# A decoder layer on one core: self-attention's output projection as three float32r products, in two parts around the transpositions, with values and query units in another order

## The reference

```
# self-attention: 16 query heads of 128, one key/value head, causal, rotary
xn = layernorm(x) * gamma                        # x: (32, 56, 256)
q  = rotary(xn @ Wq) * 128 ** -0.5               # 16 heads of 128
k, v = rotary((xn @ Wkv)[..., :128]), (xn @ Wkv)[..., 128:]
x2 = x + softmax(causal(q @ k.T)) @ v @ Wo       # Wo: (2048, 256), the projection changed here
# cross-attention: 16 heads of 16 over 1500 masked rows, then its own projection
x3 = x2 + norm(cross(layernorm(x2), context)) ...
# feed-forward: three quantised products, 256 -> 1024 (two, gated) -> 256
```

## Time and profile before

| | |
|---|---|
| median of three runs | 1445.63 us |
| the profiled execution | 1444.34 us |
| its span, first to last instruction | 1442.4 us |
| mean granted TensorE clock | 0.980 of full speed |
| TensorE busy | 1376.7 us |
| VectorE busy | 1013.8 us |
| ScalarE busy | 716.9 us |
| GpSimd busy | 447.3 us |

### The profile page before, as it was taken

How to read it: one execution, slowest core, us unless ns; L and a number is a source line. 1 busy time by engine, 2 the same in 40 slices (tenths; PEclk the granted TensorE clock), 3 DMA queues, 4 the chain that set the end, 5 groups by cost and what they waited for, 6 DMA issues and landing times.

```text
span 1442.4 us, 54968 instructions
## 1 busy us (share of the span) xinstructions
PE 1376.7 (95%) x25094; PEld 1176.8 (82%) x25094; DVE 1013.8 (70%) x1792; ACT 716.9 (50%) x939; POOL 447.3 (31%) x400
## 2 busy tenths in 40 slices
PE   5899999998899999999999999999999999999983
PEld 5687787786688888888888888888888888888872
DVE  4676676666136787786777777687878778677765
ACT  3445445444255645555555555555554555555540
POOL 4332333222222333333324233233333333332400
PEclk9999999999899999999999999999999999999995
DMA  9100001000111121111112121111212121121100
GB/s 260 23 1 31 1 1 31 1 30 1 58 49 57 31 77 44 56 58 46 58 37 63 31 77 52 57 49 45 64 31 77 41 62 55 45 61 34 49 2 7
DMA packets 38808, 66.75 MB, mean 46 GB/s; under 512 B 3605, under 2 KB 36818, under 8 KB 38578
## 3 DMA queue, kind: packets, MB, share of 16 engines
q1 hardware_dynamic: 38578, 63.24, 15.1%
HBM read 61.40 MB, written 1.84 MB: 44 GB/s over the span
## 4 chain that ended last, share of the span: by engine, by line
PE 71%; DVE 2%; issue 0%; POOL 0%; POOLq 0%; DVEq 0%
PE proj_ps L1277 19%; PE proj_ps L1268 19%; PE score_ps L1295 14%; PE sum_ps L1315 12%; PE side_ps L1350 2%; PE side_ps L1332 2%; PE side_ps L1364 1%; PE side_ps L1357 1%; PE side_ps L1339 0%; DVE inv L1109 0%; DVE exps L1097 0%; DVE amax L1150 0%; DVE hidden L1182 0%; DVE hidden L1193 0%; DVE sig L1192 0%
## 5 line engine op out<-in xcount | busy, mean ns | idle before, releaser
L1049 ACT ACTIVATE exps<-score_ps 125x1792 f32<-125x1792 f32 x192 | 320.5, 1669 | 419.0 <-PE score_ps L1295 419.0
L1097 DVE TENSOR_SCALAR exps<-exps,top 125x896 f32<-125x896 f32 x384 | 287.9, 791 | 18.0 <-ACT exps L1049 17.5
L1295 PE MATMUL score_ps<-spread,keys 32*125 32x112 f32 x6144 | 219.3, 279 | 0.0
L1315 PEld LDWEIGHTS sum_ps<-exps,vals 125*32 125x32 f32 x12288 | 163.0, 110 | 50.9 <-issue 34.4
L1088 DVE COPY vals<-proj_ps 125x512 f32<-125x512 f32 x192 | 128.2, 687 | 103.4 <-PE proj_ps L1277 103.0
L1295 PEld LDWEIGHTS score_ps<-spread,keys 32*125 32x125 f32 x6144 | 185.1, 183 | 15.4 <-issue 0.4
L1315 PE MATMUL sum_ps<-exps,vals 125*32 125x56 f32 x12288 | 191.5, 214 | 2.9 <-DVE exps L1097 2.9
L992 POOL TENSOR_TENSOR low<-raw_early,high 128x500 fp32r<-128x500 f32 x64 | 100.8, 1583 | 231.2 <-issue 115.4
L992 POOL TENSOR_TENSOR low_early<-raw_early,high_early 128x500 fp32r<-128x500 f32 x62 | 104.3, 1691 | 172.3 <-issue 104.1
L1041 ACT ACTIVATE keys<-proj_ps,b_k 128x500 f32<-128x500 f32 x192 | 129.9, 677 | 52.4 <-PE proj_ps L1268 52.4
L286 POOL TENSOR_TENSOR swapped<-swapped,sin 128x448 f32<-128x448 f32 (+1 forms) x72 | 88.6, 1232 | 138.5 <-ACT swapped L507 138.5
(11 more groups left out here) (156 smaller groups left out, 2411.6 us busy)
## 6 DMA issues: line engine op xcount, KB each, us to landing
raw_early<-in_ctxT SPq DMA_DIRECT2D x64, 500.0 KB, 4.0
raw<-in_ctxT SPq DMA_DIRECT2D x32, 500.0 KB, 3.5
w_q<-in_attn_Wq SPq DMA_DIRECT2D x4, 512.0 KB, 8.1
w_o<-in_attn_Wo SPq DMA_DIRECT2D x1, 2048.0 KB, 21.5
out<-y_out SPq DMA_DIRECT2D x16, 112.0 KB, 1.9
rows<-in_x SPq DMA_DIRECT2D x1, 1344.0 KB, 16.8
raw_early<-in_ffn_gate_wT SPq DMA_DIRECT2D x1, 1024.0 KB, 9.6
raw_early<-in_ffn_val_wT SPq DMA_DIRECT2D x1, 1024.0 KB, 5.1
```

The lines of the kernel that those rows point to most:

```text
L1049: nc.scalar.activation(exps[t % 2][:, :, :, :].rearrange("p h r n -> p r h n"), score_ps[0:TILE, :, 0:2 * QW].rearrange("p r (h n) -> p r ...
L1097: nc.vector.tensor_scalar(tile, tile, LIMIT_LO, top[:, n, at:at + 1], ALU.max, ALU.min)\
L1295: ins = nc.tensor.matmul(score_ps[0:TILE, r, to:to + HE * S], keys[c % 2][32 * r:32 * r + 32, k, (at + half) * TILE:(at + half + 1) * TILE ...
L1315: ins = nc.tensor.matmul(sum_ps[32 * h:32 * h + VW, g, :], vals[c % 2][:, at + half, HJ * g + h, :], exps[t % 2][:, half, r, col:col + S], ...
```

## The change

The output projection is computed from two parts of each operand. ScalarE copies `out_ps` to `outT_h` in float32r; VectorE subtracts that from `out_ps` and writes the rest as `outT_l` (`out_low`, four a pair). The weights are split in the same way into `w_oh` and `w_ol`, in two halves of eight heads, through the buffer that later holds the feed-forward weights (`out_weights`). `out_rows` then issues three float32r products for each head, 48 in all, and in the pairs with query units the first eight heads come ahead of `turn(p,0)` and the other eight behind it.

The order in a pair is new. `norm_turn`, q2 and q3 come behind `turn(p,1)` on TensorE; on ScalarE both `out_half(p,0,·)` and `probs_out(p,1)` come ahead of `normed_out` and the swaps of q2 and q3; on VectorE the first two `out_low` come ahead of q2's rotation. Pair 0 keeps q2 and q3 ahead of its transpositions.

To make room in SBUF, `masked` is gone (the masked scores are written into `probs`), there are three `swapped` buffers instead of four, `w_f` lies in the first half of `raw_early` and is loaded and split at pair 13 instead of 15, and five tiles of the feed-forward part are allocated and loaded in `block_b` (their reader waits for `late_in`). The diff, cut to its core:

```diff
-        w_o = sb("w_o", [P, AH, D])
+        w_oh = sb("w_oh", [P, AH, D], F32R)
+        w_ol = sb("w_ol", [P, AH, D], F32R)
...
-        masked = sb("masked", [P, AU, 2, S])
-        outT = sb("outT", [P, AH, ROWS])
+        outT_h = sb("outT_h", [P, AH, ROWS], F32R)
+        outT_l = sb("outT_l", [P, AH, ROWS], F32R)
...
             units += more[0:1]
             if p >= 2:
                 units += [("xq", p - 2)]
-            if j and g + 2 < GROUPS:
-                units += [("norm", g + 2)]
             units += more[1:2]
             if p in TOTALS:
                 units += [("total", TOTALS.index(p))]
             if p:
                 units += [("y", p - 1)]
+            if j and g + 2 < GROUPS:
+                units += [("norm", g + 2)]
             units += more[2:4]
             if p:
...
+            def out_weights(n):
+                sp.dma_start(w_raw[:, :].rearrange("p (h n) -> p h n", h=half_o),
+                             dram["attn_Wo"].rearrange("(h p) n -> p h n", p=P)[:, half_o * n:half_o * (n + 1), :])\
+                  .then_inc(wo_in[n], 16)
+
+            out_weights(0)
             sp.dma_start(w_xq[:, :, :], dram["xattn_WqT"].rearrange("(c p) n -> p c n", p=P)).then_inc(small2_in, 16)
             sp.dma_start(b_xq[:, :], dram["xattn_bq"]).then_inc(small2_in, 16)
+            sp.wait_ge(w_o_split, 1)
+            out_weights(1)
+            sp.wait_ge(early_zero, 2)
+            for to, of in early.loads(dram):
+                sp.dma_start(to, of).then_inc(early_in, 16)
+            sp.wait_ge(w_o_split, 2)
             for n, (src, how, _) in enumerate(W):
                 if n:
                     sp.wait_ge(raw_used, n)
                 c = src.shape[0] // P
                 sp.dma_start(w_raw[:, :].rearrange("p (c n) -> p c n", c=c), src.rearrange(how, p=P))\
                   .then_inc(raw_in[n], 16)
-                if n == 0:
-                    for k, name in enumerate(("xattn_WkT", "xattn_WvT")):
-                        sp.dma_start(early.w_f[:, k, :, :], dram[name].rearrange("(c p) n -> p c n", p=P))\
-                          .then_inc(early_w_in, 16)
-                    sp.wait_ge(early_zero, 2)
-                    for to, of in early.loads(dram):
-                        sp.dma_start(to, of).then_inc(early_in, 16)
             sp.wait_ge(raw_used, 3)
+            for k, name in enumerate(("xattn_WkT", "xattn_WvT")):
+                sp.dma_start(early.w_f[:, k, :, :], dram[name].rearrange("(c p) n -> p c n", p=P)).then_inc(early_w_in, 16)
+            sp.wait_ge(early_w_split, 2)
             for c in range(2):
                 sp.dma_start(early.ring(c), context_chunk(dram, c)).then_inc(early_ctx_in[c], 16)
...
+            def out_low(p, k, b):
+
+                dve.wait_ge(outT_high, 2 * (2 * p + k) + b + 1)
+                nc.vector.tensor_tensor(outT_l[:, AU * k:AU * (k + 1), b * S:(b + 1) * S],
+                                        out_ps[:, b, 0:AU * S].rearrange("p (h s) -> p h s", s=S),
+                                        outT_h[:, AU * k:AU * (k + 1), b * S:(b + 1) * S].bitcast(F32),
+                                        ALU.subtract).then_inc(outT_ready, 1)
+
+            def out_weights(n):
+
+                dve.wait_ge(w_o_high, n + 1)
+                nc.vector.tensor_tensor(w_ol[:, half_o * n:half_o * (n + 1), :].rearrange("p h n -> p (h n)"), w_raw[:, :],
+                                        w_oh[:, half_o * n:half_o * (n + 1), :].rearrange("p h n -> p (h n)").bitcast(F32),
+                                        ALU.subtract).then_inc(w_o_split, 1)
 
             def residual(p):
...
+            out_weights(0)
...
                 normalise(p)
                 for name in more[1:2]:
                     rotary(name)
+                if p == 0:
+                    out_weights(1)
                 if j == 0 and g + 2 < GROUPS:
...
+                if p == WEIGHTS_AT:
+                    early.weights_low(nc, dve, early_w_high, early_w_split)
                 if p:
                     residual(p - 1)
-                for name in more[2:3]:
+                for name in more[2:3] if p == 0 else ():
+                    rotary(name)
+                for b in range(2):
+                    out_low(p, 0, b)
+                for name in more[2:3] if p else ():
                     rotary(name)
                 if p:
                     norm2_rows(p - 1)
                 for name in more[3:4]:
                     rotary(name)
+                for b in range(2):
+                    out_low(p, 1, b)
                 if j and g + 2 < GROUPS:
                     rotary(("kv", g + 2))
...
-                if r >= 4:
-                    act.wait_ge(rot_ready, r - 3)
-                nc.scalar.copy(swapped[r % 4][0:64, 0:w], bank(name)[64:128, 0:w])
-                ins = nc.scalar.copy(swapped[r % 4][64:128, 0:w], bank(name)[0:64, 0:w])
+                if r >= 3:
+                    act.wait_ge(rot_ready, r - 2)
+                nc.scalar.copy(swapped[r % 3][0:64, 0:w], bank(name)[64:128, 0:w])
...
             def out_half(p, k, b):
 
                 act.wait_ge(pv_done, 2 * p + k + 1)
-                ins = nc.scalar.copy(outT[:, AU * k:AU * (k + 1), b * S:(b + 1) * S],
-                                     out_ps[:, b, 0:AU * S].rearrange("p (h s) -> p h s", s=S))
-                ins.then_inc(outT_ready, 1)
+                nc.scalar.copy(outT_h[:, AU * k:AU * (k + 1), b * S:(b + 1) * S],
+                               out_ps[:, b, 0:AU * S].rearrange("p (h s) -> p h s", s=S)).then_inc(outT_high, 1)
+
+            def out_weights(n):
+
+                act.wait_ge(wo_in[n], 16)
+                nc.scalar.copy(w_oh[:, half_o * n:half_o * (n + 1), :].rearrange("p h n -> p (h n)"), w_raw[:, :])\
+                  .then_inc(w_o_high, 1)
 
             def normed2_out(p):
...
             swap(("kv", 1))
+            out_weights(0)
             act.wait_ge(small2_in, 16 * SMALL2)
             for p in range(PAIRS):
...
+                if p == 0:
+                    out_weights(1)
+                if p == WEIGHTS_AT:
+                    early.weights_high(nc, act, early_w_in, early_w_high)
                 if p == PAIRS - 1:
-                    early.split_high(nc, act, early_w_in, early_w_high, early_ctx_in[0], early_high)
+                    early.split_high(nc, act, early_ctx_in[0], early_high)
+                for name in more[1:2]:
+                    swap(name)
+                for name in more[2:4] if p == 0 else ():
+                    swap(name)
+                probs_out(p, 0)
+                out_half(p, 0, 0)
+                out_half(p, 0, 1)
+                probs_out(p, 1)
                 if j and g + 2 < GROUPS:
                     normed_out(g + 2)
-                for name in more[1:2]:
-                    swap(name)
-                probs_out(p, 0)
-                for name in more[2:3]:
-                    swap(name)
-                out_half(p, 0, 0)
-                probs_out(p, 1)
-                out_half(p, 0, 1)
-                for name in more[3:4]:
+                for name in more[2:4] if p else ():
                     swap(name)
                 out_half(p, 1, 0)
...
-            def out_rows(p):
-
-                to = begin(("y", p))
-                pe.wait_ge(wo_in, 16)
-                pe.wait_ge(outT_ready, 4 * (p + 1))
-                for h in range(AH):
-                    ins = nc.tensor.matmul(to[0:ROWS, 0:D], outT[:, h, :], w_o[:, h, :], start=(h == 0),
-                                           stop=(h == AH - 1))
-                ins.then_inc(unit_filled, 1)
+            def out_rows(p, first, last):
+
+                if first == 0:
+                    begin(("y", p))
+                    pe.wait_ge(w_o_split, 2)
+                    pe.wait_ge(outT_ready, 4 * (p + 1))
+                to = bank(("y", p))
+                for h in range(first, last):
+                    for n, (part, w) in enumerate(((outT_h, w_oh), (outT_h, w_ol), (outT_l, w_oh))):
+                        ins = nc.tensor.matmul(to[0:ROWS, 0:D], part[:, h, :], w[:, h, :], start=(h == 0 and n == 0),
+                                               stop=(h == AH - 1 and n == 2))
+                if last == AH:
+                    ins.then_inc(unit_filled, 1)
 
...
-                if j and g + 2 < GROUPS:
-                    norm_turn(g + 2)
                 for u in more[1:2]:
                     heads_q(g + 1, u)
                 if p in TOTALS:
                     total(TOTALS.index(p))
-                if p:
-                    out_rows(p - 1)
                 if p == 0:
                     for u in more[2:4]:
                         heads_q(g + 1, u)
+                if p:
+                    out_rows(p - 1, 0, half_o if more else AH)
                 turn(p, 0)
-                for u in more[2:3] if p else ():
-                    heads_q(g + 1, u)
+                if p and more:
```

(43 more changed lines are left out.)

36 lines of the change are left out of this document (19 added, 17 removed).

## The result

The changed kernel takes 1468.3 us (median of 4 runs, 1463.46 to 1468.98) against 1445.19 (4 runs) for the kernel before: a ratio of 1.015, 95% interval 1.0125 to 1.0176. It is slower. The forecast was 1465.

A forecast was written before the change was run, and what follows sets the result against it. TensorE, 95% busy, was taken to set the pace. Terms 8.0 + 2.1 + 8.5 + 2.8 - 0.5 - 1.6 = +19.3 us on 1444.3 gave 1463.6, median 1465 us; range 1443 to 1473.

The forecast's parts named there:

- the collision: GpSimd's q3 sine takes the shared port ahead of VectorE's `norm2_rows`: 0.84 us a pair, bounds 0 and 1.15; chance 0.50.
- the start: Pair 0: splitting the output weights and the load between delay pair 1's scores, +8.0 us (5 to 11).
- the sum: Whole span: start, pairs and last product together, with the port delay, give +19.3 us.
- The projection: TensorE's `out_rows`: 48 float32r products take 6.06 us in place of 7.0, 0.94 us a pair less.
- Wait A: Ahead of `turn(p,0)` in an even pair: TensorE stands 0.6 us for the probabilities.
- Wait B: Ahead of `norm2_turn(p-1)`: TensorE stands 0.9 us for the normed rows behind q2's rotation, before any port delay.
- The pairs: Steady pairs with the port delay: even 21.1 us, odd 23.3, so 44.4 for two against 42.7.
- a rival of 0.05: TensorE's clock falls in each pair, up to 3.4 us a time: 1480 us for five, 1509 for all; chance 0.05.
- The gain that I put at nothing: Steady pairs: the shorter product gives nothing, two pairs staying at 42.7 us before the port delay.

The follow-up runs named there:

- ten_heads: Changed kernel with the projection cut behind ten heads in place of eight: 1463.42 us, ratio 1.0131 to the kernel before.
- sine_waits: Changed kernel with GpSimd's sine of q3 waiting until `norm2_rows` is written, VectorE's order kept: 1454.04 us, ratio 1.0077.
- norm2_first: Changed kernel with `norm2_rows` moved ahead of q2's rotation on VectorE: 1448.05 us, ratio 1.0025.
- order_alone: Changed kernel's new order with the 16 float32 products of before, undivided `w_o` and no `out_low`: 1473.47 us, ratio 1.0193.
- woven_total: woven_start with the `total` unit behind the norm unit and the middle part of the quantising behind `norm2_rows`: 1432.34 us, ratio 0.9905.
- low_first: products_alone with the first two `out_low` and `norm2_rows` ahead of q2's rotation, both `out_half(p,0)` ahead of `probs_out(p,1)`: 1448.96 us, ratio 1.0019.
- start_later: Changed kernel with VectorE's first weight split behind pair 0's division and both engines' second split at that pair's end: 1470.71 us, ratio 1.0187.
- products_alone: Changed kernel with three products in the order of before, the first `out_low` behind `norm2_rows`: 1465.99 us, ratio 1.0145.
- woven: Changed kernel with q2 between `turn(p,0)` and the projection's second part, cut behind head 10, and q2 swapped and rotated earlier: 1451.05 us, ratio 1.0037.
- woven_start: woven with the output weights split later and TensorE waiting for their second half only at head 8: 1446.2 us, ratio 1.0014.
- combined: low_first with the norm unit behind `turn(p,1)`, its bank behind q2's, and the late weight splits of woven_start: 1438.09 us, ratio 0.9945.

## Why the prediction was right

The waits, the collision and the start came as the forecast had them; the sum was 5.5 us short for the span, and most of that is the clock.

*The projection.* Forecast 6.06 us. The second half lasts from 228.74 to 231.74, 3.0 us, so 6.0. The row was the right price.

*Wait A.* Forecast 0.6 us, measured 0.57 (228.33); ten_heads takes it away and its 0.7 us goes.

*Wait B and the port.* From q2's start to `norm2_turn` 5.94 us were forecast, 5.1 and 0.84, and 5.95 are measured (210.43 to 216.38). The sine was to ask 4.4 us behind q2's start and came at 4.38; `norm2_rows`, forecast at 4.57, came at 4.58. sine_waits takes the collision alone away and norm2_first takes both.

By the Trainium skill (SBUF — State Buffer, SBUF: two separate sides) the holder keeps the port for its whole instruction. The traces agree that one engine waits for the other, nearly to the end: `norm2_rows` ends 0.15 us behind the sine (216.23, 216.08), less than the 0.41 us that it takes alone. The Trainium skill leaves open which of two waiters comes next; here GpSimd, whose sine starts 0.20 us ahead of `norm2_rows` in the trace (214.81, 215.01), came first, each of 12 times.

*The pairs.* Forecast 21.1 and 23.3, measured 21.05 and 23.12.

*The start*, in order of time (ScalarE's and VectorE's splits, then TensorE):

```profile
36.23 1.90 ACT L574 CAST w_oh<-raw_early 128x2048 fp32r<-128x2048 f32 x1
...
38.16 2.29 DVE L427 TENSOR_TENSOR w_ol<-raw_early,w_oh 128x2048 fp32r<-128x2048 f32 x1 [0.16 <-ACT w_oh L574]
...
40.37 1.08 DVE L396 TENSOR_TENSOR probs<-a_score_ps,causal 128x896 f32<-128x896 f32 x1
...
40.48 0.37 SPq L255 DMA_DIRECT2D raw_early<-in_attn_Wo  x1
...
46.29 1.90 ACT L574 CAST w_oh<-raw_early 128x2048 fp32r<-128x2048 f32 x1 [1.49 <-DMA raw_early<-in_attn_Wo]
...
51.98 3.22 DVE L427 TENSOR_TENSOR w_ol<-raw_early,w_oh 128x2048 fp32r<-128x2048 f32 x1
...
52.07 1.87 PE L724 MATMUL out_ps<-probsT,values 64*128 64x448 f32 x4 [3.71 <-ACT probsT L562]
...
58.36 1.86 PE L724 MATMUL out_ps<-probsT,values 64*128 64x448 f32 x4 [3.38 <-DVE outT_l L419]
```

The mask came at 40.37 (forecast 40.7), the load's wait ended at 46.29 (46.6), `out_heads(0,0)` came at 52.07 (52.3) and `out_heads(0,1)` at 58.36 (58.1). The scores of pair 1 started at 60.16 (59.9), behind ScalarE's, GpSimd's and VectorE's queues as named. The second subtraction, 3.22 us against 2.44, was held by sines.

*What was mis-sized: the clock.* The sum gave +19.3 us for the span, and +24.8 came. To the scores of pair 2 it was 11.1 (forecast 8.0 + 2.1); ten pairs brought 10.6 (8.5), pairs 12 and 13 4.5 (2.8), and the rest -1.4 (-2.1). The clock fell for 3.4 us at 283.4, 307.3 and 331.2. Pairs 10 to 13 took 21.21, 25.50, 21.62 and 22.18 us, 4.2 more than 3 x 21.06 + 23.12. I had the fall as a rival of 0.05 for at least five pairs; it came three times. I had argued against it from the last pairs, which stand 0.6 and 1.15 us at the full clock. That holds for pair 14 of the kernel before. In its pair 15 TensorE stood 0.62, 1.15 and 0.91 us, and the clock was low right behind that:

```profile
358.30:365.10 6.80, 6.27 (x20) 5.06 (x20) 1.85 (x6) 0.94 (x3) 1.25 (x1) 0.50 0.00 0
```

So the record spoke less against the rival than I said, and the sum should have had a term for it. That the fall follows from wait B is supported by ten_heads and order_alone, where wait B is whole and the falls are more, and by norm2_first and sine_waits, where it is gone or 0.97 us and there are none. This is support and not proof: each of these traces is one execution. What decides in which pairs it falls is not settled either: the four runs differ by 5.5 us, with mean clocks of 0.971 to 0.976.

*What I had not looked at.* The gain that I put at nothing could be had. In woven_total two pairs take 40.0 to 40.6 us in place of 42.7. The forecast priced the order that was there, and that only.

## What to carry to other kernels

When work is taken from the busiest engine, list each chain on the others that this work covered, with the time at which each ends; the shorter work pays only if every one is moved with it. A moved unit also moves its sine or copy on an engine that shares a port, and everything behind it in a ring of three banks: write out who holds each bank in every pair, the ones with an extra unit too. Start a change of precision with the splitting of its weights: here it put 8 us at the start, and 4.9 came back by placing it later.

## What the runs showed of the hardware

- Of two waiters, the GpSimd sine that had waited went ahead of VectorE's next instruction, at 0.81 us a time.
- The subtraction from PSUM of 448 columns to float32r took 0.62 us as `by_cos` does (46 of mean 617 ns in the changed kernel, none beside a sine). In low_first 25 of the 64 ran beside a sine, and they took the same 0.61 to 0.63 us.
- TensorE's clock fell to 1.2 GHz, mostly for 3.4 us at a time, in some of the pairs in which it had stood 1.8 us or more at once (the changed kernel, start_later, order_alone, ten_heads, products_alone, low_first, woven, woven_start). In pairs 2 to 13 of norm2_first, sine_waits, woven_total and combined, whose longest waits are 1.5, 1.0, 1.1 and 1.5 us, it did not fall. The longest wait alone doesn't decide: in pair 14 of woven_total and combined, where it was 1.3 us, the clock fell for 6.8 us. A fall of 3.4 us cost about 1.4 to 1.5 us (4.2 for the three of the changed kernel, 1.53 in an odd pair of ten_heads).
